# Attention values by split single-pass products on five of eight key tiles, and an unsplit key product

## The chip, the cores and the metric

The kernel runs on one core of one Trainium2 chip. Times are device microseconds (us) of one execution. The time before is 673.21 us, the median of 3 runs (672.68 to 674.67).

## The reference, cut to what matters

The computation is one gated cross-attention block and one feed-forward block. The change touches the attention alone:

```python
q_hk = (hidden_q @ Wq.T).reshape(b, s, H, K)              # hidden_q is the layer norm of x
q_big = jnp.einsum('bshk,hkq->bshq', q_hk, w_kc_q)
kv_rope = kv_c * cos[None] + _rotate_half(kv_c) * sin[None]
q_r = jnp.einsum('bshq,hqr->bhsr', q_big, W_qr)
k_r = jnp.einsum('bld,hdr->bhlr', kv_rope, W_kr)           # the key product
scores = jnp.einsum('bhsr,bhlr->bhsl', q_r, k_r)
attn = jax.nn.softmax(scores, axis=-1)
ctx_c = jnp.einsum('bhsl,bld->bhsd', attn, kv_rope)        # the value product
ctx_lat = jnp.einsum('bhsd,hkd->bshk', ctx_c, w_kc_kv)
out = ctx_lat.reshape(b, s, H * K) @ Wo.T
```

There are 2 batches of 512 queries and 1024 keys, 16 heads, a key and value width of 128. The feed-forward part that follows has quantized weights of 512 x 2048 and runs in FP8 and BF16.

## The kernel before

**Pairs, units, steps.** Heads are taken two at a time: eight pairs, p = 0 to 7. A pair has four units, w = 0 to 3: unit w serves batch w // 2 and one half of its queries. A unit has eight steps, c = 0 to 7. In step c TensorE multiplies key tile c (128 keys) of the softmax by the values (`pv_matmul`), and adds it into one PSUM bank, `ps_ctx` for even units and one bank of `ps_b` for odd ones. Between the steps lie the side tasks of `SIDE`: `m` and `a` make the next pair's query matrix, `q` its queries, `k` its keys (`k_hi`, `k_lo`), `b` the pair's output matrix, and `out` applies it. All orders are written out by hand, one queue for each engine. An engine works its queue strictly in order, and semaphores order the engines among themselves.

**One unit's softmax runs ahead.** For a unit two or three units ahead, PE makes the scores of query tiles t = 2, 3 in step 1 and of t = 0, 1 in step 5 (`score_matmuls`). For each tile VectorE (DVE) takes the maximum from PSUM (`max_tile`), ScalarE (ACT) the exponential into `E` (`exp_tile`), DVE the reciprocal of the row sum (`inv_tile`), GpSimd (POOL) scales the tile (`pool_scale`), and DVE turns its 32 x 32 blocks in place (`turn_blocks`). Scores for two more tiles can be written only when both exponentials of the last two are done. When a unit's four tiles are turned, SyncE (SP) issues 16 transfers that exchange partition groups from `E` to `G` (`exchange`). `G` then holds the turned softmax, the moving operand of `pv_matmul`. The buffers `E`, `G` and the result banks have two places, for even and odd units.

**Two ways to multiply float32.** PE multiplies plain float32 in one instruction of the program, which the trace shows as two records. The other way splits each operand x into a high part, x rounded to the one-pass format fp32r, and a low part x - high, and adds three one-pass products: high by high, high by low, low by high. ACT copies out the high part, and DVE (for PSUM) or POOL (for SBUF) subtracts for the low part. Scores, outputs, the keys (`k`) and in pairs 1 to 4 the queries (`q`) are split. The value product, `m`, `a` and `b` are plain.

**Names.** `ctx_high` and `ctx_low` split a unit's result. `side_high` and `side_low` split a side task's. `wk_high` and `wk_low` split the key weights and `kvT_hi`, `kvT_lo` are the split transposed values, used for the keys. In pairs 0 to 3 ACT also sums the absolute values of the feed-forward weights (`sum_half`, one half at steps 1 and 4). From unit 1 of pair 4 it takes two halves' tanh in step 0 (`tanh_half`), and DVE rounds them in steps 3 and 4 (`round_half`). I call pairs 0 to 3 the summing pairs and pairs 4 to 6 the rounding pairs. In pair 0 POOL makes the low parts of the layer-normed input (`xn_low`, four halves), for which PE waits before pair 1; in pairs 4 and 5 it joins them again (`join_xn`).

Of the kernel before, what the change touches and what calls it, by code (L numbers as in the profile page):

```python
# [99 lines left out]
WK_AT = (0, 1)  # L100
# [81 lines left out]
def build(nc, A):  # L182
    with ExitStack() as ctx:
# [947 lines left out]
        def _(sp):  # L1131
# [35 lines left out]
        def xn_low(pool, b):  # L1167

            pool.wait_ge(side_done, side_index(0, "first", ("q", b)) + 1)
            for i in (2 * b, 2 * b + 1):  # L1170
                hi, lo, full = xn_half(i)
                pool.wait_ge(xn_high, i + 1)
                nc.gpsimd.tensor_tensor(lo, full, hi.bitcast(F32), ALU.subtract).then_inc(xn_split, 1)

        def join_xn(pool, b):
# [2 lines left out]
            for h in range(2):
                hi, lo, _ = xn_half(2 * b + h)
                whole = xn_rows[:, b, h * DT // 2:(h + 1) * DT // 2, :].rearrange("p c s -> p (c s)")  # L1180
                nc.gpsimd.tensor_tensor(whole, hi.bitcast(F32), lo.bitcast(F32), ALU.add).then_inc(xn_joined, 1)

        def pool_pair(pool, p, last=False):
            for w in range(4):
                second, first = not (last and w >= 2), not (last and w >= 1)
                for at, t in enumerate((1, 2, 3, 0)):
                    if second if t else first:
                        pool_scale(pool, *unit_ahead(p, w, 2 if t else 3), t)
                    if at == 0:
                        if is0(p) and w in XN_LOW_SLOTS:  # L1190
                            xn_low(pool, XN_LOW_SLOTS.index(w))
                        for b in range(BATCH):
                            if isinstance(p, int) and (p, w) == XN_JOIN_SLOTS[b]:
                                join_xn(pool, b)
                    if last and (w, at) == (1, 2):
                        ln2_root(pool, 0)
                if last and w == 1:
                    atanh_end(pool)
# [8 lines left out]
        @block.gpsimd
        def _(pool):
# [788 lines left out]
```

## Time and profile before

| | before |
|---|---|
| median of the runs | 673.21 us |
| profiled execution | 677.15 us, span 675.4 us |
| mean granted TensorE clock | 0.995 |
| busy: PE, DVE, ACT, POOL | 653.5, 543.9, 356.8, 259.7 us |

Times below are counted in us from the start of the span. A matmul record overlaps the next one, so what a matmul costs is read from start to start. ACT's and DVE's records overlap the next by about 0.1 us as well. A pair starts with its first value tile, just ahead of task `m`: `m` of pairs 1 to 6 starts at 116.99, 182.95, 248.93, 316.5, 383.13 and 451.25. The feed-forward part begins about 561.

### The profile page before, as it was taken

The page shows a single profiled execution, that of the slowest core. Times are in us where ns is not written, and L with a number is a line of the kernel's source. Part 1 is how long each engine was busy: PE and PEld are TensorE (multiplying, and loading weights), DVE is VectorE, ACT ScalarE, POOL GpSimd, SP SyncE. Part 2 cuts the span into 40 slices and gives each one's busy share as a digit, 9 for nine tenths or more (in the row PEclk, how much of TensorE's full clock was granted, in tenths as well). Part 3 has the DMA queues.
Part 4 walks back from the last instruction along what each step waited for, and adds up shares of the span by engine and source line. Part 5 has one row for each costly group of instructions (what it writes and reads, how often), then busy time and mean ns, then how long its engine had stood idle before and what let it go on. Part 6 is the DMA issues. An engine that isn't in the chain of part 4 may idle for free.

```text
span 675.4 us, 9297 instructions
## 1 busy us (share of the span) xinstructions
PE 653.5 (97%) x2870; PEld 377.5 (56%) x2870; DVE 543.9 (81%) x882; ACT 356.8 (53%) x571; POOL 259.7 (38%) x232
## 2 busy tenths in 40 slices
PE   9798999999999999999999999999999898999997
PEld 8564555665665555565655555555555454445553
DVE  5787877788868885888698979997999886998873
ACT  3564664455445544554545454545454533498875
POOL 4822265133223222322235443332333352686651
PEclk9999999999999999999999999999999998999999
DMA  8108885788498849884988688869688763000001
GB/s 299 63 1 218 234 226 117 226 237 228 108 241 243 220 105 243 231 215 109 239 245 207 184 225 237 212 168 238 163 214 230 172 149 101 1 0 32 17 33 48
DMA packets 45206, 112.77 MB, mean 167 GB/s; under 512 B 11888, under 2 KB 15088, under 8 KB 45040
## 3 DMA queue, kind: packets, MB, share of 16 engines
q1 hardware_dynamic: 43712, 110.01, 61.5%
q10 hardware_dynamic: 1392, 2.29, 1.0%
q8 instruction: 19, 0.31, 0.2%
q14 instruction: 19, 0.16, 0.1%
q0 software_dynamic: 64, 0.00, 0.0%
HBM read 45.16 MB, written 2.10 MB: 70 GB/s over the span
## 4 chain that ended last, share of the span: by engine, by line
PE 48%; DVE 30%; ACT 7%; SPq 6%; POOL 3%; issue 3%; DMA 2%; PEld 1%; POOLq 0%; DVEq 0%; ACTq 0%; PEldq 0%
DVE E L1765 9%; PE ps_b L1392 9%; PE ps_s L1371 7%; DVE small L1755 7%; PE ps_ctx L1392 7%; ACT E L1580 6%; SPq L1096 5%; PE ps_s L586 5%; DVE wq L1781 2%; PE ps_b L1265 2%; POOL E L1160 2%; DVE x_sb L1745 2%; PE ps_b L1267 2%; PE ps_b L637 2%; PE ps_b L1266 2%
## 5 line engine op out<-in xcount | busy, mean ns | idle before, releaser
L1160 POOL TENSOR_SCALAR E<-E,small 128x1024 f32<-128x1024 f32 x128 | 151.1, 1190 | 346.7 <-DVE small L1760 346.6
L1580 ACT ACTIVATE E<-ps_s,small 128x1024 f32<-128x1024 f32 x128 | 142.3, 1113 | 209.0 <-DVE small L1755 177.5
L1765 DVE STREAM_TRANSPOSE E<-E 128x1024 f32<-128x1024 f32 x124 | 152.8, 1233 | 27.9 <-POOL E L1160 27.8
L1755 DVE TENSOR_REDUCE small<-ps_s 128x1 f32<-128x1024 f32 x128 | 149.1, 1203 | 4.5 <-PE ps_s L1371 4.4
L1392 PE MATMUL ps_ctx<-G,kv 128*128 128x512 f32 x256 | 123.2, 599 | 0.0
L1392 PE MATMUL ps_b<-G,kv 128*128 128x512 f32 x256 | 119.9, 598 | 2.1 <-DMA G<-E 2.1
L1392 PEld LDWEIGHTS ps_b<-G,kv 128*128 128x128 f32 x256 | 48.0, 190 | 51.8 <-issue 46.0
L1392 PEld LDWEIGHTS ps_ctx<-G,kv 128*128 128x128 f32 x256 | 46.4, 189 | 43.0 <-issue 40.3
L1265 PE MATMUL ps_b<-b_hi,ctx_hi 128*128 128x512 f32 x128 | 66.4, 519 | 0.6 <-DVE ctx_lo L1717 0.6
L1371 PE MATMUL ps_s<-k_hi,q_hi 64*128 64x512 f32 x256 | 57.3, 443 | 4.6 <-ACT E L1580 3.6
L586 PE MATMUL ps_s<-wq,q12T 128*128 128x512 fp8e4 x256 | 61.1, 385 | 0.1
L1371 PE MATMUL ps_s<-k_hi,q_lo 64*128 64x512 f32 x256 | 51.1, 393 | 0.0
L1371 PE MATMUL ps_s<-k_lo,q_hi 64*128 64x512 f32 x256 | 50.8, 392 | 0.0
L1267 PE MATMUL ps_b<-b_lo,ctx_hi 128*128 128x512 f32 x128 | 50.4, 393 | 0.0
L1266 PE MATMUL ps_b<-b_hi,ctx_lo 128*128 128x512 f32 x128 | 50.2, 392 | 0.0
L524 POOL TENSOR_TENSOR hg<-h_f,E 128x512 f32<-128x512 f32 x32 | 40.4, 1270 | 25.1 <-DVE h_f L932 25.1
L1745 DVE SCALAR_TENSOR_TENSOR x_sb<-ps_b,small,x_sb 128x512 f32<-128x512 f32 x62 | 44.6, 720 | 4.7 <-PE ps_b L1267 4.7
L1760 DVE RECIPROCAL small<-small 128x1 f32<-128x1 f32 x128 | 19.3, 156 | 31.0 <-ACT E L1580 24.7
L1371 PEld LDWEIGHTS ps_s<-k_hi,q_hi 64*128 64x128 f32 x256 | 24.1, 183 | 32.6 <-issue 19.1
L586 PEld LDWEIGHTS ps_s<-wq,q12T 128*128 128x128 bf16 x256 | 24.4, 99 | 28.3 <-issue 4.1
L1265 PEld LDWEIGHTS ps_b<-b_hi,ctx_hi 128*128 128x128 f32 x128 | 24.0, 188 | 23.1 <-issue 15.3
L1266 PEld LDWEIGHTS ps_b<-b_hi,ctx_lo 128*128 128x128 f32 x128 | 24.1, 189 | 10.5 <-issue 7.7
(199 smaller groups left out, 960.9 us busy)
## 6 DMA issues: line engine op xcount, KB each, us to landing
G<-E SPq DMA_DIRECT2D x496, 128.0 KB, 2.4
w_stage<-in_wffn SPq DMA_DIRECT2D x48, 512.0 KB, 4.4
wo_s<-in_woT SPq DMA_DIRECT2D x8, 512.0 KB, 5.3
wq_s<-in_wq SPq DMA_DIRECT2D x7, 512.0 KB, 6.3
wkcq_s<-in_wkcqT SPq DMA_DIRECT2D x7, 384.0 KB, 4.5
out<-x_sb SPq DMA_DIRECT2D x8, 256.0 KB, 2.0
x_sb<-in_x SPq DMA_DIRECT2D x3, 512.0 KB, 5.9
wqr_s<-in_wqr SPq DMA_DIRECT2D x7, 192.0 KB, 5.4
```

What stands on the lines that cost most here:

```text
L524: nc.gpsimd.tensor_tensor(hg[:, k, cols], h_f[:, k, cols], g3[:, cols], ALU.mult).then_inc(hg_done, 1)
L586: last = nc.tensor.matmul(ps_s4[:, 2 * i + c % 2, :], q12T[:, k, i, d, :], wq8[:, DT * i + d, cols], start=(d == 0), stop=(d == DT - 1))
L1160: nc.gpsimd.tensor_scalar(e, e, rowinv[:, k:k + 1], 1.0, ALU.mult, ALU.mult).then_inc(scaled, 1)
L1265: nc.tensor.matmul(into, ctx_hi[:, cols], b_hi[:, h, :], start=(h == 0), stop=False)
L1266: nc.tensor.matmul(into, ctx_lo[:, cols], b_hi[:, h, :], start=False, stop=False)
L1267: last = nc.tensor.matmul(into, ctx_hi[:, cols], b_lo[:, h, :], start=False, stop=(h == 1))
L1371: last = nc.tensor.matmul(ps_s[:, h, cols], q[head, b, rows], k[head, b, cols], start=(i == 0), stop=(i == 2))
L1392: last = nc.tensor.matmul(CTX_PS[w % 2].rearrange("p (t i q) -> p t i q", t=ST, i=4), kv[:, w // 2, c, :], turned, start=(c == 0), stop=(c ...
L1580: nc.scalar.activation(out, scores, ACT.Exp, bias=negmax[:, k:k + 1], accum_out=rowsum[:, k:k + 1]).then_inc(exp_done, 1)
L1745: last = nc.vector.scalar_tensor_tensor(x, bank_in, g_tanh[:, 0:1], x, ALU.mult, ALU.add)
L1755: nc.vector.tensor_reduce(negmax[:, k:k + 1], ps_s[:, t % 2, :], AX_X, ALU.max, negate=True).then_inc(max_done, 1)
L1765: nc.vector.transpose(e_tile(w % 2, t), e_tile(w % 2, t)).then_inc(blocks_turned, 1)
```

## The change

Five of the eight value tiles of a unit (`SPLIT = 5`, tiles 0 to 4) are multiplied as three one-pass products in pairs 0 to 6. The values' parts `kv_hi`, `kv_lo` are cut once by POOL in the prologue. The softmax's high part is copied by ACT (`split_high`) into one of three places of `g_hi`, and POOL (`split_low`) puts the low part into the memory of `G` itself. PE takes the tiles in the order of `STEP_TILE`, so that each unit opens with a plain tile. Pair 7 takes all tiles plain, for which POOL adds the values together again (`join_kv`). The key product becomes plain, so the split of `kvT` and of the key weights falls away (one `wk` copy on ACT and one subtraction on DVE in a pair, four subtractions on DVE in the prologue), and the next key weights are loaded later. `xn_low` and `join_xn` are taken one half at a time, at the end of a unit's POOL work.

```diff
+SPLIT = 5
+HIGH_PLACE = (0, 2, 1, 0, 1)
+STEP_TILE = (5, 0, 6, 1, 2, 3, 7, 4)
+HIGH_STEPS = (0, 0, 0, 2, 4)
-WK_AT = (0, 1)
-XN_AT = ((1, 1), (1, 4), (2, 1), (2, 4))
-XN_LOW_SLOTS = (2, 3)
+XN_AT = ((1, 1), (1, 5), (2, 1), (2, 5))
+XN_LOW_SLOTS = (1, 2, 3, 3)
-XN_JOIN_SLOTS = ((4, 2), (5, 0))
+XN_JOIN_SLOTS = ((4, 2), (4, 3), (5, 0), (5, 0))
...
+        def split_low(pool, p, w, i):
+            tile = g_tile(w % 2, i)
+            pool.wait_ge(split_hi, SPLIT * 4 * p + (SPLIT * w + i + 1))
+            pool.sem_inc(pool_passed, 1)
+            nc.gpsimd.tensor_tensor(g_tile(w % 2, i, G_lo), tile, high_part(i).bitcast(F32).rearrange("p (t i q) -> p t i q", t=ST, i=4),
+                                    ALU.subtract).then_inc(split_lo, 1)
...
+                u2, u3 = unit_ahead(p, w, 2), unit_ahead(p, w, 3)
+                if is0(p) and w == 0:
+                    split_low(pool, p, w, 0)
+                if second:
+                    pool_scale(pool, *u2, 1)
...
+                if not (last or is0(p) and w == 0):
+                    split_low(pool, p, w, 0)
+                if not last:
+                    split_low(pool, p, w, 1)
...
+                if not last:
+                    split_low(pool, p, w, 2)
+                if second:
+                    pool_scale(pool, *u2, 2)
+                    pool_scale(pool, *u2, 3)
...
+                    split_low(pool, p, w, 3)
...
+                    split_low(pool, p, w, 4)
+                for i in range(2 * BATCH):
+                    if is0(p) and w == XN_LOW_SLOTS[i]:
+                        xn_low(pool, i)
+                    if isinstance(p, int) and (p, w) == XN_JOIN_SLOTS[i]:
+                        join_xn(pool, i)
+                if isinstance(p, int) and (p, w) == (PAIRS - 2, 3):
+                    join_kv(pool, 0)
+                if first:
+                    pool_scale(pool, *u3, 0)
...
-                nc.tensor.matmul(into, wh, kvT_hi[:, b, cols], start=True, stop=False)
-                nc.tensor.matmul(into, wl, kvT_hi[:, b, cols], start=False, stop=False)
-                last = nc.tensor.matmul(into, wh, kvT_lo[:, b, cols], start=False, stop=True)
+                last = nc.tensor.matmul(into, wkr_s[:, :, :].rearrange("p a r -> p (a r)"), kvT[:, b, cols], start=True, stop=True)
...
+            if tile < SPLIT and not (isinstance(p, int) and p == PAIRS - 1):
+                high = high_part(tile).rearrange("p (t i q) -> p t i q", t=ST, i=4)
+                pe.wait_ge(split_lo, SPLIT * 4 * p + (SPLIT * w + tile + 1))
+                nc.tensor.matmul(into, kv_hi[:, b, tile, :], high, start=(c == 0), stop=False)
+                nc.tensor.matmul(into, kv_lo[:, b, tile, :], high, start=False, stop=False)
+                last = nc.tensor.matmul(into, kv_hi[:, b, tile, :], g_tile(w % 2, tile, G_lo), start=False, stop=(c == LT - 1))
+                if tile < SPLIT - 1:
+                    last.then_inc(split_done, 1)
+            else:
+                last = nc.tensor.matmul(into, kv[:, b, tile, :], turned, start=(c == 0), stop=(c == LT - 1))
...
+        def split_high(act, p, w, i):
+            used = 4 * (SPLIT - 1) * p + (SPLIT - 1) * w
+            if i == 0:
+                if is0(p) and w == 0:
+                    act.wait_ge(kv_cut, 6)
+                else:
+                    act.wait_ge(split_done, used)
+                act.wait_ge(exchanged[w % 2], 2 * EXCHANGE * p + EXCHANGE * (w // 2 + 1))
+            elif i == 2:
+                if not (is0(p) and w == 0):
+                    act.wait_ge(pv_done, 4 * p + w)
+            elif i == 3:
+                act.wait_ge(split_done, used + 1)
+            elif i == 4:
+                act.wait_ge(split_done, used + 3)
+            copy_act(high_part(i).rearrange("p (t i q) -> p t i q", t=ST, i=4), g_tile(w % 2, i)).then_inc(split_hi, 1)
...
+                    if c == 0 and variant != "last":
+                        split_high(act, p, w, 0)
                     if c == 0 and w:
                         ctx_high(act, p, w - 1)
...
-                    if (w, c) == WK_AT and variant != "last":
-                        wk_high(act, 16 * p + 32)
+                    for i in range(1, SPLIT):
+                        if c == HIGH_STEPS[i] and variant != "last":
+                            split_high(act, p, w, i)
```

ACT's queue around the start of unit 2 of pair 4, before. `ctx_hi` is the result of unit 1, the first `k_hi` the last key task of unit 1, `w_stage` the two tanh halves, the second `k_hi` the key task of step 0, `E` the four exponentials of the unit, and the last `ctx_hi` opens unit 3:

```order
L1536 ACTIVATE ctx_hi<-ps_b 128x512
L1536 ACTIVATE k_hi<-ps_b 128x512
L1604 ACTIVATE w_stage<-w_stage,small 128x1024 x2
L1536 ACTIVATE k_hi<-ps_b 128x512
L1580 ACTIVATE E,small<-ps_s,small 128x2x4x128 x4
L1536 ACTIVATE ctx_hi<-ps_ctx 128x512
```

The same place in the changed kernel:

```order
L1615 ACTIVATE g_hi<-G 128x512
L1615 ACTIVATE ctx_hi<-ps_b 128x512
L1615 ACTIVATE k_hi<-ps_b 128x512
L1615 ACTIVATE g_hi<-G 128x512 x2
L1698 ACTIVATE w_stage<-w_stage,small 128x1024 x2
L1615 ACTIVATE k_hi<-ps_b 128x512
L1674 ACTIVATE E,small<-ps_s,small 128x2x4x128
L1615 ACTIVATE g_hi<-G 128x512
L1674 ACTIVATE E,small<-ps_s,small 128x2x4x128
L1615 ACTIVATE g_hi<-G 128x512
L1674 ACTIVATE E,small<-ps_s,small 128x2x4x128 x2
```

Three copies now stand ahead of the tanh halves and so of the second `k_hi`, and one stands between the exponentials of query tiles 2 and 3.

POOL's queue from the middle of pair 0 to its end, before. `xnT` are the low parts of the input, `E` the scalings, and the branch opens the loop over pairs 1 to 3:

```order
L1160 TENSOR_SCALAR E<-E,small 128x4x256 x14
L1173 TENSOR_TENSOR xnT<-xn_rows,xnT 128x1024 x2
L1160 TENSOR_SCALAR E<-E,small 128x4x256 x4
L1173 TENSOR_TENSOR xnT<-xnT_full,xnT 128x1024 x2
L1160 TENSOR_SCALAR E<-E,small 128x4x256 x3
L1253 UNCONDITIONAL_BRANCH
```

In the changed kernel, units 2 (end) and 3 of pair 0:

```order
L1194 TENSOR_TENSOR xnT<-xn_rows,xnT 128x1024
L1182 TENSOR_SCALAR E<-E,small 128x4x256 x2
L1226 TENSOR_TENSOR G_lo<-G,g_hi 128x4x4x32 x3
L1182 TENSOR_SCALAR E<-E,small 128x4x256 x2
L1226 TENSOR_TENSOR G_lo<-G,g_hi 128x4x4x32 x2
L1194 TENSOR_TENSOR xnT<-xnT_full,xnT 128x1024 x2
L1182 TENSOR_SCALAR E<-E,small 128x4x256
L1324 UNCONDITIONAL_BRANCH
```

The last two low parts of the input, which stood ahead of three scalings of unit 3, now stand behind two of them and behind the unit's five value-tile subtractions.

## Rows read from the trace of the kernel before

**Rows 1.** Windows, pairs 2 and 5: busy PE, PEld, DVE, ACT, POOL; granted clock; DMA.

```profile
182.95:248.93 65.98, 65.98 (x279) 39.77 (x278) 52.51 (x73) 32.41 (x58) 17.84 (x17) 1.00 0.78 203
383.13:451.25 68.12, 67.96 (x269) 37.97 (x268) 58.91 (x81) 34.54 (x57) 25.81 (x19) 1.00 0.80 213
```

**Rows 2.** Chain that ended last, pair 2: start us, us, what.

```profile
226.38 1.59 PE ps_s L1371 x12
```

**Rows 3.** The same chain, pair 5, unit 2.

```profile
424.49 1.14 DVE small L1755
...
425.66 2.35 ACT E L1580 x4
...
428.03 0.06 DVE small L1760
```

**Rows 4.** Timeline of PE, pair 2: plain value tiles, then split query products.

```profile
229.40 2.73 PE L1392 MATMUL ps_ctx<-G,kv 128*128 128x512 f32 x6
...
231.97 1.02 PE L1392 MATMUL ps_b<-G,kv 128*128 128x512 f32 x2
...
233.06 0.40 PE L1345 MATMUL ps_b<-xnT,a_lo 128*128 128x512 f32 x1
...
235.34 0.39 PE L1346 MATMUL ps_b<-xnT,a_hi 128*128 128x512 f32 x1
```

**Rows 5.** Timeline of ACT, pair 5: copies.

```profile
401.65 0.60 ACT L1536 ACTIVATE ctx_hi<-ps_ctx 128x512 fp32r<-128x512 f32 x1
...
402.12 0.61 ACT L1536 ACTIVATE b_hi<-ps_b 128x512 fp32r<-128x512 f32 x1
...
422.59 0.58 ACT L1536 ACTIVATE k_hi<-ps_b 128x512 fp32r<-128x512 f32 x1
```

**Rows 6.** Timeline of DVE, pair 5.

```profile
387.89 0.42 DVE L1717 TENSOR_TENSOR wk_lo<-wkr_s,wk_hi 128x128 fp32r<-128x128 f32 x1
...
411.58 0.16 DVE L1760 RECIPROCAL small<-small 128x1 f32<-128x1 f32 x1
...
411.74 1.36 DVE L1781 TENSOR_SCALAR wq<-w_stage 128x1024 fp8e4<-128x1024 f32 x1
...
423.84 0.65 DVE L1717 TENSOR_TENSOR k_lo<-ps_b,k_hi 128x512 fp32r<-128x512 f32 x1
...
427.05 0.69 DVE L1781 TENSOR_SCALAR wq<-w_stage 128x1024 fp8e4<-128x1024 f32 x1
...
428.03 0.16 DVE L1760 RECIPROCAL small<-small 128x1 f32<-128x1 f32 x1 [0.28 <-ACT E L1580]
```

**Rows 7.** Timelines of ACT and PE, pair 2 (first row) and pair 3.

```profile
224.74 1.12 ACT L1580 ACTIVATE E<-ps_s,small 128x1024 f32<-128x1024 f32 x1
...
265.22 1.11 ACT L1580 ACTIVATE E<-ps_s,small 128x1024 f32<-128x1024 f32 x1 [7.47 <-DMA G<-E]
...
268.79 0.50 PE L1344 MATMUL ps_b<-xnT,a_hi 128*128 128x512 f32 x1 [1.10 <-DVE b_lo L1717]
...
292.38 1.12 ACT L1580 ACTIVATE E<-ps_s,small 128x1024 f32<-128x1024 f32 x1
...
293.65 0.50 PE L1371 MATMUL ps_s<-k_hi,q_hi 64*128 64x512 f32 x2
```

**Rows 8.** Groups of POOL and ACT by form: busy us, mean ns, idle before.

```profile
L524 POOL TENSOR_TENSOR hg<-h_f,E 128x512 f32<-128x512 f32 x32 | 40.4, 1270 | 25.1 <-DVE h_f L932 25.1
...
L1173 POOL TENSOR_TENSOR xnT<-xnT_full,xnT 128x1024 fp32r<-128x1024 f32 x2 | 4.7, 2375 | 1.6 <-PE ps_b L1341 1.6
...
L1536 ACT ACTIVATE xnT<-xn_rows 128x1024 fp32r<-128x1024 f32 x2 | 2.1, 1052 | 0.0
```

**Rows 9.** Timelines of PE and ACT in pair 0, and the chain at its end.

```profile
52.05 0.50 PE L1371 MATMUL ps_s<-k_hi,q_hi 64*128 64x512 f32 x2 [0.37 <-ACT E L1580]
...
107.79 1.11 ACT L1580 ACTIVATE E<-ps_s,small 128x1024 f32<-128x1024 f32 x1
...
116.13 0.86 PE ps_ctx L1392 x2
```

More of the change, by code:

```diff
@@ L1124, in sp_pair @@
                     load_wq(sp, p + 2)
-                    sp.wait_ge(wk_ready, p + 2)
+                if w == 2 and not (variant == "last" or isinstance(p, int) and p == 6):
+                    sp.wait_ge(side_done, side_index(p, variant, ("k", 1, 1)) + 1)
                     load_kr(sp, p + 2)
@@ L1165, in xn_half, with xn_low @@
             return tuple(x.rearrange("p c s -> p (c s)") for x in (XNT[b][:, 0, part, :], XNT[b][:, 1, part, :], XNT_FULL[b][:, part, :]))
[L1167 to L1175, printed above, removed]
-            pool.wait_ge(side_done, side_index(XN_JOIN_PAIR, "mid", ("q", b)) + 1)
[L1178 to L1181, printed above, removed]
+        def xn_low(pool, i):
+            pool.wait_ge(side_done, side_index(0, "first", ("q", i // 2)) + 1)
+            hi, lo, full = xn_half(i)
+            pool.wait_ge(xn_high, i + 1)
+            nc.gpsimd.tensor_tensor(lo, full, hi.bitcast(F32), ALU.subtract).then_inc(xn_split, 1)
@@ L1185, in pool_pair @@
                 second, first = not (last and w >= 2), not (last and w >= 1)
[L1186 to L1198, printed above, removed]
+                u2, u3 = unit_ahead(p, w, 2), unit_ahead(p, w, 3)
[3 more added lines that the diff above has]
+                    pool_scale(pool, *u2, 1)
+                if last and w == 0:
+                    join_kv(pool, 1)
+                if not (last or is0(p) and w == 0):
+                    split_low(pool, p, w, 0)
+                if not last:
+                    split_low(pool, p, w, 1)
+                if last and w >= 2:
+                    ln2_root(pool, w - 2)
+                if last and w == 3:
+                    rms_root(pool, 1)
+                if not last:
[3 more added lines that the diff above has]
+                    pool_scale(pool, *u2, 3)
                 if last and w == 2:
@@ L1248, in _ @@
                 pool_scale(pool, 0, 0, t)
-            for t in range(ST):
-                pool_scale(pool, 0, 1, t)
+            cut_kv(pool, 0)
+            pool_scale(pool, 0, 1, 0)
+            pool_scale(pool, 0, 1, 1)
+            cut_kv(pool, 1)
+            pool_scale(pool, 0, 1, 2)
+            pool_scale(pool, 0, 1, 3)
             pool_scale(pool, 0, 2, 0)
@@ L1315, in side_matmuls @@
                 _, b, j = task
-                pe.wait_ge(wk_ready, 1 if at is not None else p + 2)
+                pe.wait_ge(ld_kr, 16 if at is not None else 16 * p + 32)
                 if at is not None:
@@ L1821, in dve_pair @@
                         inv_tile(dve, *u3, 0)
-                    if (w, c) == WK_AT and variant != "last":
-                        wk_low(dve, p + 2)
                     if variant == "last":
```

87 lines of the change are left out of this document (50 added, 37 removed).

## The prediction

> **What bounds the kernel now.** I read the busy times of whole pairs first. PE is busy for 65.98 of 65.98 us in summing pair 2, and for 67.96 of 68.12 in rounding pair 5 [rows 1], at a granted clock of 1.00, the level of 2.4 GHz. That looks like one bound for the whole attention. Yet a busy share does not say who waits for whom, and DVE rises from 52.51 to 58.91 us between the two pairs.
>
> So I read the chain that ended last. In pair 2 it is PE work alone, one matmul group behind the other [rows 2]. In pair 5 hardly a matmul stands in it: maximum on DVE, exponentials on ACT, reciprocal on DVE, then rounding and turning on DVE [rows 3]. The reader should see that 0.28 us of DVE's waiting ahead of a reciprocal is for an exponential of ACT [rows 6], while PE, the busiest engine, sets nothing there. From about 329 to 547 us the chain keeps that shape. The kernel thus has two regimes: pairs 0 to 3 (to 316) by PE, pairs 4 to 7 by the softmax chain through DVE and ACT.
>
> Last I looked for how much room the softmax chain has in the PE regime. In pair 3 the exponentials of the step 6 scores wait 7.47 us for the exchange of unit 1, and behind them PE waits 1.10 us for `b_lo` at 268.79. In unit 2 the exponential that starts at 292.38 ends at 293.50, and the scores that need its bank start at 293.65. In pair 2 the same exponential ends at 225.86 and the scores start at 226.31. The room is 0.15 and 0.45 us [rows 2, 7].
>
> **PE's own account.** Six records of plain tiles, three products, take 231.97 - 229.40 = 2.57 us, 0.857 each. Ten steps of split products take 235.34 - 233.06 = 2.28, 0.228 each, so 0.684 for three [rows 4]. A split product saves 0.173 us. There are 5 x 28 = 140 of them, 24.2 us. The plain key product costs 0.173 more, 32 times: 5.5. PE's work falls by 18.7 us, 2.8 in a pair. The low part is read from `G` in pieces of 32 columns. Plain tiles are read in the same pieces, at 0.214 us for each 512-column quarter, so I charge nothing for it.
>
> The Trainium skill, page "Perfetto Trace Analysis", section "Identifying the Most-Contended Engine", says to find the bottleneck by occupancy and to optimize that engine first, with a warning that matmul busy share is a poor measure. By the plain rule the sum would be 673.2 - 18.7 = 654.5. The chain's row decides against it for pairs 4 to 6.
>
> **What is added elsewhere.** ACT gets 140 copies. A copy of 512 columns costs 0.47 from start to start [rows 5], and one of 1024 from SBUF 1.05 [rows 8]: I take 0.5. POOL gets 140 subtractions of 1.27 [rows 8]. Both engines have the time: 32 to 35 us and 18 to 26 us of 66 to 68 are busy [rows 1], and 10 and 25 come on top. What counts is where they stand.
>
> *Rounding pairs.* The copy of tile 3 stands between the exponentials of query tiles 2 and 3. In unit 2 DVE waits for the second one already, so all 0.5 goes into the chain. In unit 1 the reciprocal at 411.58 follows rounding at once [rows 6] and the exponential ends just then, so 0.5 there too, and by the same pattern in unit 3. In unit 0 it is 0.5 less the `wk_lo` that goes, a record of 0.42 [rows 6] that overlaps the next by the usual 0.1: 0.15 to 0.2. Three more copies stand ahead of the tanh halves, and ACT comes to `k_hi` or `q_hi` 1.5 us later. `k_hi` ends at 423.17 [rows 5] and `k_lo` takes it at 423.84 [rows 6], 0.67 of room: DVE stalls 0.8, and the maxima stand behind it. Unit 3 repeats this with `q_hi` and `q_lo`. In unit 1 the query product itself ends later than that, in unit 0 there is no such task. A pair: 0.15 + 0.5 + 1.3 + 1.3 = 3.25 us. Pair 4 has no tanh in unit 0, and its exchange covers that unit: 3.1. In unit 0 of pair 5 two joins of 2.4 each [rows 8] stand ahead of a scaling and nearly fit: 0.3. Together 3.1 + 3.55 + 3.25 = 9.9. What PE saves here only becomes waiting.
>
> *Summing pairs 1 to 3.* From the landing of unit 1's exchange (265.2) a DVE chain runs to the scores of unit 2 at 293.65, with 0.15 us of room at the end. PE gets ready earlier there, but can't start earlier. Behind that point lie two split tiles of unit 2 and five of unit 3 before the next pair: 7 x 0.173 = 1.2 saved. The copy in unit 2 costs 0.5 less the room of 0.15 to 0.45, and unit 3's room takes most of its own. Pair 3: 0.6 saved. Pairs 1 and 2 have more room: 1.1 each. Together 2.8.
>
> *Pair 0.* In unit 0 tile 0 comes ahead of the scores, which now start at 52.05 [rows 9]. It needs ACT's copy behind exponentials that end about 52.0, a subtraction and three products: 0.5 + 1.3 + 0.7 = 2.5 us later. Bounds are 0 and 2.5. The next exponentials of that unit wait for the exchange anyway, as in pair 3, so I take half, 1.3. At the end, PE may not enter pair 1 before the last `xn_low`. The last exponential of unit 3 ends at 108.9 [rows 9], now 1.3 + 0.5 + 0.5 later, 111.2. Reciprocal and scaling end at 112.5, two subtractions at 115.0, two `xn_low` of 2.4 at 119.8. PE enters at 116.13 now: 3.7 us lost in pair 0, the 1.3 included.
>
> *The rest.* In the prologue `cut_kv` is six POOL operations of 640 columns, by the rate of 1.27 for 512 at most 1.6 each, in two gaps of POOL ahead of scalings; the four `kvT_lo` go, and four plain key products come. I put zero, with 1 us either way. Pair 7 has no copies. `join_kv`, up to 1.6 us on POOL twice, lies ahead of scalings that wait for exponentials: zero.
>
> **Sum:** 3.7 - 2.8 + 9.9 = 10.8 us. The profiled execution took 677.15 (span 675.4), and would take 688. The median of the runs is 3.9 lower, and on it the forecast is 684.0. Since nearly all of it is latency, its own range is 678 to 690: less if half the copies on the chain are covered, more if pair 0's opening is not.
>
> **Rivals.**
> *PE stays the bound and gains (faster).* If the chain has more room than I read, so that the copies cost nothing, pairs 0 to 3 gain about 2.3 each, 9, and pairs 4 to 6 stay: 664. It decides where the room ahead of the scores in unit 2 exceeds 0.5 + 0.5 us, PE's saving and the copy; the 0.15 of rows 7 speaks against it, PE's full busy time for it. All of 18.7 gained would be 654.5. Chance 0.27, a third of it below 664.
> *The two sides cancel.* The entry of pair 1 is not delayed and the copies cost half: -2.8 + 5 is 675. Chance 0.08 within 0.3%.
> *The port.* Rounding takes 0.69 alone and 1.36 beside a POOL scaling [rows 6]. If POOL's subtractions meet the first rounding of each unit too, 11 roundings grow by 0.67, and some turn into POOL delays: 7 more, 691. Against it: the three subtractions ahead of the scaling should be over by then. The Trainium skill, page "SBUF — State Buffer", section "Who interferes with whom", has the pair of ports taken for a whole instruction, and two-input DVE operations from SBUF meet POOL's reads too; the rows agree as to rounding. Chance 0.10, together with a slower read of the low parts.
> *The forecast:* 0.55.
>
> **How the numbers follow.** What a measurement of this kernel can tell from no change is about 0.3%, 2 us. Slower: 0.55 + 0.10 = 0.65; same 0.08; faster 0.27. The range from 664 to 690 leaves out a tenth on each side.
>
> **What the profile would show.** Right: PE idle of several us in each of pairs 4 to 6, before scores, released by ACT's exponentials; these pairs 71 us long; `k_lo` waiting for `k_hi` in unit 2; PE idle about 3 us where pair 1 opens, waiting for POOL's `xnT`; key products of 0.857 and split ones of 0.23. Wrong: pairs 4 to 6 at 68 or shorter, or pairs 1 to 3 below 64. The forecast fails if ACT reaches the copies before the exponentials are ready, or if the queue has slack that the overlapping records hide.

## The result, and the profile after

| | before | after |
|---|---|---|
| median of the runs | 673.11 us (4 runs, 672.68 to 674.67) | 686.43 us (4 runs, 685.49 to 688.11) |
| ratio | | 1.0196, 95% interval 1.0168 to 1.0225 |
| profiled execution | 677.15 us, span 675.4 | 685.49 us, span 683.7 |
| mean granted clock of the executions, here and below | 0.994 to 1.00 | 0.982 to 0.99 |

The change costs 13.3 us. A second measurement of the changed kernel, below, gave 1.0184 (1.0154 to 1.0213).

The page of the changed kernel: busy times (share of the span, instructions), the engines' shares of the chain that ended last, and five of the costliest groups (busy us, mean ns, idle time ahead and its releaser).

```profile
PE 643.2 (94%) x2978; PEld 398.7 (58%) x2978; DVE 536.9 (79%) x870; ACT 425.3 (62%) x703; POOL 443.3 (65%) x380
...
DVE 37%; PE 21%; ACT 17%; issue 13%; POOL 7%; SPq 3%; DMA 1%; DVEq 0%; POOLq 0%; PEld 0%; ACTq 0%
...
L1226 POOL TENSOR_TENSOR G_lo<-G,g_hi 128x512 fp32r<-128x512 f32 x140 | 176.8, 1291 | 0.4 <-ACT g_hi L1615 0.4
...
L1615 ACT ACTIVATE g_hi<-G 128x512 fp32r<-128x512 f32 x140 | 84.6, 628 | 0.6
L1438 PE MATMUL ps_s<-k_hi,q_hi 64*128 64x512 f32 x256 | 57.9, 447 | 14.2 <-ACT E L1674 13.2
...
L1472 PE MATMUL ps_ctx<-G,kv 128*128 128x512 f32 x116 | 59.8, 609 | 3.5 <-POOL xnT L1194 3.2
...
L1466 PE MATMUL ps_ctx<-g_hi,kv_hi 128*128 128x512 f32 x70 | 42.4, 605 | 8.5 <-POOL G_lo L1226 8.2
```

From the page of the kernel before, the row of the scores:

```profile
L1371 PE MATMUL ps_s<-k_hi,q_hi 64*128 64x512 f32 x256 | 57.3, 443 | 4.6 <-ACT E L1580 3.6
```

PE's busy time fell by 10.3 us (653.5 before), and the span grew by 8.3. PE is still busy for 94% of it, but only 21% of the chain is PE's, where it was 48%. PE now idles 14.2 us ahead of scores instead of 4.6, nearly all of it for ACT's exponentials, and 8.5 ahead of split tiles for POOL's low parts.

The windows of pairs 0 to 2 and 5 (columns as in [rows 1]):

```profile
48.30:124.83 76.53, 67.63 (x277) 41.05 (x275) 54.60 (x73) 50.78 (x91) 54.22 (x43) 0.94 0.68 176
124.83:190.47 65.64, 64.55 (x294) 43.08 (x293) 51.09 (x70) 39.74 (x72) 40.86 (x35) 0.99 0.78 205
190.47:255.83 65.36, 63.87 (x293) 42.58 (x292) 52.02 (x71) 41.88 (x78) 42.86 (x37) 1.00 0.80 205
390.01:459.71 69.70, 65.92 (x285) 40.99 (x284) 57.28 (x79) 43.76 (x74) 50.56 (x39) 1.00 0.79 208
```

Pair 2 took 65.98 us with PE always busy [rows 1]; now it takes 65.36 with 1.5 idle. Pair 5 took 68.12, now 69.70 with 3.8 idle. Pair 0 is the bad one: 76.53, with 8.9 idle and a granted clock of 0.94.

From the start of each pair's first `m` record to the next one's (the last column to the first record of the feed-forward part's matmuls), in us, one profiled execution each. The kernels from the third row on are those of the experiments:

| kernel | pair 0 | 1 | 2 | 3 | 4 | 5 | 6 and 7 |
|---|---|---|---|---|---|---|---|
| before | 68.4 | 66.0 | 66.0 | 67.6 | 66.8 | 68.1 | 110.7 |
| after | 76.5 | 65.6 | 65.4 | 66.3 | 67.9 | 69.7 | 112.2 |
| changed_again | 76.1 | 66.4 | 65.3 | 66.2 | 67.9 | 69.7 | 112.6 |
| copy_behind | 74.7 | 65.6 | 64.6 | 65.7 | 67.6 | 69.0 | 111.5 |
| copies_after_k | 74.9 | 65.2 | 65.3 | 66.1 | 66.6 | 68.1 | 111.0 |
| late_xn_wait | 71.4 | 67.6 | 65.3 | 66.2 | 67.9 | 69.7 | 113.2 |
| open_tile6 | 70.5 | 66.2 | 65.5 | 66.4 | 67.9 | 70.3 | 113.1 |
| open_filled | 75.0 | 67.5 | 65.3 | 66.2 | 67.9 | 70.2 | 112.8 |
| rounding_plain | 75.0 | 66.4 | 65.3 | 66.2 | 66.6 | 68.0 | 110.8 |
| key_alone | 68.8 | 66.6 | 66.6 | 66.8 | 67.4 | 68.3 | 111.5 |
| all_four | 67.4 | 67.6 | 66.0 | 65.8 | 66.5 | 67.5 | 110.0 |
| combo_round_plain | 67.4 | 67.7 | 64.8 | 65.7 | 66.6 | 68.0 | 111.3 |
| five | 67.8 | 65.3 | 64.7 | 65.8 | 66.4 | 67.6 | 109.9 |
| copy_between | 68.6 | 66.2 | 65.4 | 66.1 | 66.7 | 68.1 | 110.4 |

Rows that leave a pair alone differ there by up to 2 us in pairs 0 and 1 and by some tenths elsewhere; that is how finely the table can be read.

**Pair 0's opening.** Timeline of PE in the changed kernel: the plain tile 5, tile 0, then the scores (start us, us, ..., idle before and releaser).

```profile
49.64 1.02 PE L1472 MATMUL ps_ctx<-G,kv 128*128 128x512 f32 x2
53.90 0.55 PE L1466 MATMUL ps_ctx<-g_hi,kv_hi 128*128 128x512 f32 x1 [3.24 <-POOL G_lo L1226]
...
55.24 0.80 PE L1438 MATMUL ps_s<-k_hi,q_hi 64*128 64x512 f32 x2
55.83 0.63 PE L1438 MATMUL ps_s<-k_lo,q_hi 64*128 64x512 f32 x2
```

The scores start 3.19 us later than the 52.05 of [rows 9], and behind the gap every score step takes 0.43 us from start to start instead of 0.23: the granted clock is at its 1.2 GHz level there.

The next exponentials on ACT, before and in the changed kernel, and a second wait of PE in the same unit, for the low part of tile 3:

```profile
64.55 1.11 ACT L1580 ACTIVATE E<-ps_s,small 128x1024 f32<-128x1024 f32 x1 [5.81 <-DMA G<-E]
```

```profile
67.77 1.11 ACT L1674 ACTIVATE E<-ps_s,small 128x1024 f32<-128x1024 f32 x1 [4.03 <-DVE small L1847]
```

```profile
66.60 0.50 PE L1466 MATMUL ps_ctx<-g_hi,kv_hi 128*128 128x512 f32 x1 [1.95 <-POOL G_lo L1226]
```

**Pair 0's end.** The same timeline, and POOL's row for the last low parts of the input.

```profile
119.41 0.40 PE L1468 MATMUL ps_b<-G_lo,kv_hi 128*128 128x512 f32 x1
122.97 2.07 PE L1472 MATMUL ps_ctx<-G,kv 128*128 128x512 f32 x2 [3.16 <-POOL xnT L1194]
124.83 2.01 PE L1372 MATMUL ps_b<-wqr_s,wkcq_s 128*128 128x128 f32 x12
```

```profile
117.95 4.68 POOL L1194 TENSOR_TENSOR xnT<-xnT_full,xnT 128x1024 fp32r<-128x1024 f32 x2
```

Again PE is slow behind the gap: a plain tile takes 1.86 us to the next start instead of 0.857.

**Rounding pairs.** Timeline of DVE, unit 2 of pair 5, the place of [rows 3, 6].

```profile
432.00 0.69 DVE L1813 TENSOR_TENSOR k_lo<-ps_b,k_hi 128x512 fp32r<-128x512 f32 x1 [0.71 <-ACT k_hi L1615]
432.61 2.35 DVE L1847 TENSOR_REDUCE small<-ps_s 128x1 f32<-128x1024 f32 x2
435.10 0.16 DVE L1852 RECIPROCAL small<-small 128x1 f32<-128x1 f32 x1
435.25 0.69 DVE L1873 TENSOR_SCALAR wq<-w_stage 128x1024 fp8e4<-128x1024 f32 x1
436.71 0.16 DVE L1852 RECIPROCAL small<-small 128x1 f32<-128x1 f32 x1 [0.77 <-ACT E L1674]
436.87 0.70 DVE L1873 TENSOR_SCALAR wq<-w_stage 128x1024 fp8e4<-128x1024 f32 x1
```

`k_lo` waits 0.71 for `k_hi`, and the second reciprocal 0.77 where it waited 0.28 [rows 6]. But the rounding behind it takes 0.70. Before, it took 1.11:

```profile
428.18 1.11 DVE L1781 TENSOR_SCALAR wq<-w_stage 128x1024 fp8e4<-128x1024 f32 x1
```

### The profile page after: what moved, and what is told of

Same layout as the page of the kernel before. It is cut to its first block, busy times and chain, and to the rows that moved or that the text cites. A ratio compares the mean times of both kernels' runs of the same rounds, so it can differ in the third digit from the quotient of the medians.

```text
span 683.7 us, 10097 instructions
## 1 busy us (share of the span) xinstructions
PE 643.2 (94%) x2978; PEld 398.7 (58%) x2978; DVE 536.9 (79%) x870; ACT 425.3 (62%) x703; POOL 443.3 (65%) x380
## 4 chain that ended last, share of the span: by engine, by line
DVE 37%; PE 21%; ACT 17%; issue 13%; POOL 7%; SPq 3%; DMA 1%; DVEq 0%; POOLq 0%; PEld 0%; ACTq 0%
DVE small L1847 12%; DVE E L1857 10%; ACT E L1674 9%; PE ps_s L607 5%; POOL E L1182 4%; DVE x_sb L1841 3%; SPq L1117 3%; ACT g_hi L1615 3%; PE ps_s L1438 2%; PE ps_b L1408 2%; PE ps_b L658 2%; ACT w_stage L1698 2%; DVE wq L1873 2%; DVE ctx_lo L1813 1%; DVE k_lo L1813 1%
## 5 line engine op out<-in xcount | busy, mean ns | idle before, releaser
L1226 POOL TENSOR_TENSOR G_lo<-G,g_hi 128x512 fp32r<-128x512 f32 x140 | 176.8, 1291 | 0.4 <-ACT g_hi L1615 0.4
L1615 ACT ACTIVATE g_hi<-G 128x512 fp32r<-128x512 f32 x140 | 84.6, 628 | 0.6
L1438 PE MATMUL ps_s<-k_hi,q_hi 64*128 64x512 f32 x256 | 57.9, 447 | 14.2 <-ACT E L1674 13.2
L1472 PE MATMUL ps_ctx<-G,kv 128*128 128x512 f32 x116 | 59.8, 609 | 3.5 <-POOL xnT L1194 3.2
L1472 PE MATMUL ps_b<-G,kv 128*128 128x512 f32 x116 | 58.7, 594 | 2.1 <-DMA G<-E 2.1
L1336 PE MATMUL ps_b<-b_hi,ctx_hi 128*128 128x512 f32 x128 | 56.7, 443 | 1.0 <-DVE ctx_lo L1813 0.5
L545 POOL TENSOR_TENSOR hg<-h_f,E 128x512 f32<-128x512 f32 x32 | 40.5, 1274 | 23.3 <-DVE h_f L953 23.3
L1438 PEld LDWEIGHTS ps_s<-k_hi,q_hi 64*128 64x128 f32 x256 | 24.5, 185 | 44.9 <-issue 22.1
L1466 PE MATMUL ps_ctx<-g_hi,kv_hi 128*128 128x512 f32 x70 | 42.4, 605 | 8.5 <-POOL G_lo L1226 8.2
L1466 PE MATMUL ps_b<-g_hi,kv_hi 128*128 128x512 f32 x70 | 42.5, 607 | 0.0
L607 PEld LDWEIGHTS ps_s<-wq,q12T 128*128 128x128 bf16 x256 | 24.1, 98 | 27.7 <-issue 3.2
```

Of the source, the lines that this page charges most:

```text
L607: last = nc.tensor.matmul(ps_s4[:, 2 * i + c % 2, :], q12T[:, k, i, d, :], wq8[:, DT * i + d, cols], start=(d == 0), stop=(d == DT - 1))
L1226: nc.gpsimd.tensor_tensor(g_tile(w % 2, i, G_lo), tile, high_part(i).bitcast(F32).rearrange("p (t i q) -> p t i q", t=ST, i=4), ALU.subtra ...
L1336: nc.tensor.matmul(into, ctx_hi[:, cols], b_hi[:, h, :], start=(h == 0), stop=False)
L1438: last = nc.tensor.matmul(ps_s[:, h, cols], q[head, b, rows], k[head, b, cols], start=(i == 0), stop=(i == 2))
L1466: nc.tensor.matmul(into, kv_hi[:, b, tile, :], high, start=(c == 0), stop=False)
L1472: last = nc.tensor.matmul(into, kv[:, b, tile, :], turned, start=(c == 0), stop=(c == LT - 1))
```

## The experiments

Where no other kernel is named, the edit is made to the changed kernel. Ratios are to the kernel before in the same session, and differences in us are differences of ratios by 673 us; each ratio is known to about 0.003, 2 us.

### The changed kernel again

No edit.

> The changed kernel itself, once more, so that the variants have it on the same chip and in the same hour: ratio 1.0196 as measured before, within its interval of 1.017 to 1.0225, pair 0 between 75 and 76.5 us long (three variants that leave it alone took 74.7 to 75.0).

Measured: 687.10 us, ratio 1.0184 (1.0154 to 1.0213). The differences below are taken from this ratio.

### The copy of tile 3 behind the exponentials

```diff
-HIGH_STEPS = (0, 0, 0, 2, 4)
+HIGH_STEPS = (0, 0, 0, 3, 4)
```

> Only the place of one copy changes: ACT takes the high part of value tile 3 behind the exponentials of query tiles 2 and 3 instead of between them (28 units). My prediction's account (copy on the chain): 0.5 us of the chain comes back in units 1 to 3 of pairs 4 to 6 and 0.15 in their units 0, 5 us, and in summing pairs 1 to 3 the wait of 0.96 us ahead of unit 2's scores shrinks by 0.5, 1.5 more: about 680, 6.5 below the 686.4 of the changed kernel. Rival (the copy was paid back): in the changed kernel's trace the second rounding of a unit takes 0.89 and 0.70 us where it took 1.36 and 1.11 before, since it no longer runs beside the scaling of tile 2. With the copy gone from its place rounding meets scaling again and grows by 0.4: only 0.1 per unit comes back, 1 us, and with the 1.5 of the summing pairs the time is about 684. The durations of the second rounding tell the two apart: 0.7 to 0.9 by the first, 1.1 to 1.36 by the rival.

Measured: 680.59 us, 1.0092 (1.0066 to 1.0118), 6.2 us less than the changed kernel. The size is that of the first theory, but the place is not. DVE in unit 2 of pair 5:

```profile
430.92 0.69 DVE L1873 TENSOR_SCALAR wq<-w_stage 128x1024 fp8e4<-128x1024 f32 x1
431.90 0.17 DVE L1852 RECIPROCAL small<-small 128x1 f32<-128x1 f32 x1 [0.28 <-ACT E L1674]
432.05 1.10 DVE L1873 TENSOR_SCALAR wq<-w_stage 128x1024 fp8e4<-128x1024 f32 x1
```

The reciprocal's wait is 0.28 again, and the second rounding 1.10 again, as the rival had it. From the first reciprocal to the end of the second rounding's issue (the next row's start, 433.07 here and 437.48 there) it takes 2.30 us, against 2.38 in the changed kernel. Against the changed kernel's second profile, pairs 4 to 7 got 2.0 us shorter, pairs 2 and 3 0.8 and 0.5. That is 3.3. Pairs 0 and 1 give 2.2 more in this execution, of which some is scatter of the clock (see the last section). So by the pairs the copy's place is worth more than the rival's 2.5 and less than the first theory's 6.5, and its 2.0 in pairs 4 to 7 are nearer to the rival's 1 than to the first theory's 5.

### The copies of tiles 1 and 2 behind k_hi and q_hi

```diff
-HIGH_STEPS = (0, 0, 0, 2, 4)
+HIGH_STEPS = (0, 1, 1, 2, 4)
```

> The copies of value tiles 1 and 2 move from step 0 to step 1 on ACT, behind the two tanh halves and behind k_hi or q_hi of step 0. My prediction's account: k_lo and q_lo wait 0.71 and 0.82 us for them in units 2 and 3 of pairs 4 to 6, and the maxima stand behind; the waits go, 2 x 0.75 x 3 = 4.5 us: about 682. Rival: the maxima would have waited anyway, for the scores or for the exchange, and the time stays at 686.4 within 1 us. A third way: low parts 1 and 2 come so late on POOL that the scaling of tile 2 is delayed, and the time rises by 1 to 3 us.

Measured: 681.41 us, 1.0112 (1.0083 to 1.0142), 4.8 us less. Pairs 4, 5 and 6 with 7 take 1.2, 1.6 and 1.6 us less, 4.4 together: the first theory's 4.5. `k_lo` no longer waits, in unit 2 of pair 5 (DVE):

```profile
426.67 0.65 DVE L1813 TENSOR_TENSOR k_lo<-ps_b,k_hi 128x512 fp32r<-128x512 f32 x1
427.24 2.34 DVE L1847 TENSOR_REDUCE small<-ps_s 128x1 f32<-128x1024 f32 x2
```

With this edit alone pairs 4 and 5 are as long as before the change (66.6 and 68.1).

### Pairs 4 to 6 with whole tiles

`split_high` and `split_low` are left out in pairs 4 to 6, and PE takes the plain product there (`splits` holds for pairs 0 to 3). The product reads the rounded high parts of the values; their low parts are left out.

```diff
-            if tile < SPLIT and not (isinstance(p, int) and p == PAIRS - 1):
+            if tile < SPLIT and splits(p):
```

> Pairs 4 to 6 take all value tiles whole again, without copies and subtractions; the low parts of the values of tiles 0 to 4 are left out there (the plain products read the rounded high parts). Pairs 0 to 3 as in the changed kernel. My prediction's account: the split costs 9.9 us in these pairs, of which the key product's saving and wk_low are a small part, so about 10 us come back: 676.5. Rival, from the two traces: pairs 4 and 5 grew only by 1.1 and 1.6 us and pairs 6 and 7 together by 1.5, so about 4 come back: 682.5.

Measured: 680.99 us, 1.0101 (1.0082 to 1.0121), 5.6 us less. The pairs themselves give 1.2, 1.7 and 1.8, 4.7 us. That is the rival's size, half of the 9.9 that I had forecast. The windows of pairs 4 and 5 (columns as in [rows 1]):

```profile
320.66:387.30 66.64, 66.64 (x274) 39.02 (x272) 57.54 (x80) 31.18 (x50) 23.89 (x19) 1.00 0.82 217
387.30:455.28 67.98, 67.98 (x266) 37.52 (x264) 58.51 (x79) 34.23 (x56) 25.87 (x19) 1.00 0.80 213
```

They are no shorter than with the copies of tiles 1 and 2 moved. But this doesn't show that these two copies are all that splitting cost the chain: with whole tiles and the plain key product PE is busy for the whole of both pairs, so here PE may be what holds them.

### Plain tile 6 ahead of tile 0 in the first unit

```diff
-            b, tile = w // 2, STEP_TILE[c]
+            b, tile = w // 2, ((5, 6, 0, 1, 2, 3, 7, 4) if is0(p) and w == 0 else STEP_TILE)[c]
```

> Only in unit 0 of pair 0 the value tiles are taken in the order 5, 6, 0 instead of 5, 0, 6, so that two plain tiles stand ahead of the scores and the scores need not wait for the low part of tile 0. Theory: the idle 3.24 us from 50.5 shrinks to at most 1, the scores start at about 52.1 instead of 55.24, and the granted clock does not fall; the unit loses 5 us against before, 3.2 by the idle time and 2 by the clock, and nearly all comes back: 682. Rival: what comes back is lost at the end of pair 0, where PE waits for the last low part of the input, whose start POOL reaches by its own chain; then the wait of 3.16 us there grows and the time falls by less than 2.

Measured: 681.51 us, 1.0100 (1.0073 to 1.0126), 5.6 us less. Timeline of PE at the opening:

```profile
51.79 0.51 PE L1438 MATMUL ps_s<-k_hi,q_hi 64*128 64x512 f32 x2 [0.32 <-ACT E L1674]
...
53.87 0.50 PE L1466 MATMUL ps_ctx<-g_hi,kv_hi 128*128 128x512 f32 x1 [0.42 <-POOL G_lo L1226]
```

Two gaps of 0.3 and 0.4 us stand in place of one of 3.24, and the score steps take 0.23. The query product of unit 1 starts 19.60 us after `m` (19.66 before, 24.89 after). A wait of 1.75 us for the low part of tile 3 stays, at 62.20, without moving the query product. The wait at the end of pair 0 stays as long as it was, 3.19 us, so the rival's return of the loss didn't come. Pair 0 is still 2.1 us longer than before the change.

### The gap at the opening filled with products

```diff
                         task_first = False
+                        wait_bank(pe, p, variant, ("a",))
+                        for _ in range(4):
+                            nc.tensor.matmul(ps_b[:, side_bank(variant, ("a",)), :]..., kv[:, 0, 5, :], g_tile(0, 5), start=True, stop=True)
                         pv_matmul(pe, p, w, c)
```

> The changed kernel with four plain products of tile 5 written to a free bank ahead of tile 0 in the first unit, so that TensorE works through its 3.24 us of waiting there (4 x 0.857 = 3.4 us); nothing else changes and their result is not used. If the loss behind the gap is the clock's: the granted clock stays at the 2.4 GHz level (1.00 in the window 48 to 60 instead of 0.72 to 0.85), the scores start at 55.3 as before but take 1.5 us instead of 2.6, the products behind them run at full speed, and pair 0 gets 2 us shorter: 684.5. If the clock has no part and only the wait counts, the time stays at 686.4.

Measured: 685.09 us, 1.0150 (1.0119 to 1.0180). That is 2.3 us under the changed kernel, with intervals that overlap. Windows of the changed kernel (second measurement), of this kernel, and of the kernel with the copies of tiles 1 and 2 moved, whose opening has a gap of 3.2 us that is not filled (length, busy PE, PEld, DVE, ACT, POOL, granted clock, DMA share, GB/s):

```profile
54.00:58.00 4.00, 4.00 (x16) 2.33 (x15) 0.20 (x1) 0.00 (x0) 2.76 (x3) 0.50 0.91 206
```

```profile
54.00:58.00 4.00, 4.00 (x27) 2.84 (x27) 2.17 (x2) 0.91 (x1) 2.78 (x3) 1.00 0.90 206
```

```profile
54.00:58.00 4.00, 4.00 (x27) 2.75 (x26) 2.07 (x2) 0.81 (x1) 2.88 (x3) 1.00 0.93 209
```

With the gap filled the clock behind it is 1.00, but in the third kernel it is 1.00 as well, with the gap. So this run doesn't show what lowers the clock. What the clock is worth can be read from the start of unit 1's query product after `m`: 24.9, 24.5, 24.3 and 24.1 us in the four executions whose clock fell right behind the gap (the changed kernel's two, copy_behind, late_xn_wait; in the first of them it fell behind the next gap as well), 23.3 and 23.4 in the two where it fell only behind the next gap (copies_after_k, rounding_plain), 23.4 here, where it fell there too. A fall at once costs 0.7 to 1.5 us more, and filling the gap brings nothing against those two. Of the 5.2 us lost in this unit, 3.6 or more are not the first fall's. The 2.3 us between the medians are within what the intervals leave open.

### The wait for the input's low parts moved to its user

```diff
-            pe.wait_ge(xn_split, 2 * BATCH)
             with pe.Fori(1, 4) as p:
...
                     else:
+                        pe.wait_ge(xn_split, 2 * BATCH)
                         for c in range(DT):
```

> PE's wait for the last low parts of the input moves from ahead of pair 1 to the query products of pairs 1 to 4, its first user, in unit 1. Theory: the idle 3.16 us ahead of pair 1 goes, and with it what the slow clock behind it cost (the first value tile 1.86 us instead of 0.86, m 1.94 instead of 1.4, some more until 128): about 5 us, 681.5. Rival: the softmax chain of pair 1 (exponentials, then the exchange) is what is late, PE only waits elsewhere, and at most 1 us comes back: 685.5 to 686.5.

Measured: 685.07 us, 1.0155 (1.0125 to 1.0184), 2.0 us less. Neither theory: pair 0 is 4.7 us shorter and pair 1 is 1.3 longer. PE's timeline in pair 1:

```profile
124.66 0.50 PE L1467 MATMUL ps_ctx<-g_hi,kv_hi 128*128 128x512 f32 x1 [2.54 <-POOL G_lo L1226]
```

PE enters pair 1 at once, and then stands for tile 0, whose low part is behind the same `xn_low` in POOL's queue. The wait moved 4 us on and shrank by 0.6.

### The plain key product alone

The kernel before, with the key product of the change and without the split of the key weights and of the transposed values. The value tiles stay plain.

> The kernel before with only the plain key product (no split of the transposed values and of the key weights, the later load of them), and no split value tiles. Account by PE work: 0.173 x 4 a pair, 0.7 us in each of the PE-bound pairs 0 to 3 and nothing in pairs 4 to 6 but the saving of wk_low (0.15 a pair): 2.8 - 0.5 = 2.3 slower, 675.5. Rival: the wk copy on ACT and subtraction on DVE were on the chain, and in the prologue four subtractions on DVE; then it is even or faster, 671 to 673.

Measured: 677.91 us, 1.0038 (1.0018 to 1.0058), 2.6 us slower, against the account's 2.3. The sum fits, but by the pairs it is not made up as the account has it. Pairs 0, 1 and 2 grow by 0.5, 0.6 and 0.6 us, near the 0.7 expected. Pair 3 gets 0.7 shorter, and pairs 4 to 7, which were to gain 0.5, grow by 1.6. In pair 5 PE is busy for 68.22 of 68.30 us.

### The four edits together

`HIGH_STEPS = (0, 1, 1, 3, 4)`, tile 6 ahead of tile 0, and the late wait for the low parts.

> The four edits together: copies of tiles 1 and 2 in step 1, the copy of tile 3 behind both exponentials, the wait for the low parts of the input at the query products, and plain tile 6 ahead of tile 0 in the first unit. If the four are independent and each returns what the account gives it (6.5, 4.5, 5, 4.5), 666; if the copies were paid back by shorter roundings and only pair 0's two waits and the summing pairs return, 686.4 - 5 - 4 - 1.5 = 676. Below 673 it beats the kernel before.

Measured: 671.36 us, 0.9958 (0.9945 to 0.9972). It is faster than the kernel before. The four edits alone sum to 18.6 us (6.2 + 4.8 + 5.6 + 2.0), together they bring 15.2.

### The four edits, and pairs 4 to 6 whole

The low parts of the values are left out in pairs 4 to 6, as above.

> The four edits together, and pairs 4 to 6 with whole value tiles (the low parts of the values of tiles 0 to 4 left out there). If the summing pairs keep PE's saving once the waits are gone, pairs 1 to 3 take 63.2 to 63.9 us instead of 66 and pair 0 about 67: 673 - 8 - 1 = 664. Rival: the summing pairs are held by the softmax chain through unit 2 and stay at 65 or more: 669 to 671.

Measured: 672.97 us, 0.9967 (0.9952 to 0.9981), not to be told from the four edits alone. Pair 2 took 64.8 and pair 1 67.7: the first theory's 63.2 to 63.9 came nowhere. In pairs 4 and 5 the four edits alone leave PE busy for 64.4 of 66.5 and 65.7 of 67.5 us, here for all of 66.6 and 68.0. So PE's saving in pairs 4 to 6 is worth 0.1 to 1.3 us in each column of the table, and nothing that the runs can tell.

### A fifth edit, and the copy put back between

```diff
                     split_low(pool, p, w, 2)
+                if is0(p) and w == 3:
+                    xn_low(pool, 2)
                 if second:
...
-                    if is0(p) and w == XN_LOW_SLOTS[i]:
+                    if is0(p) and w == XN_LOW_SLOTS[i] and i != 2:
```

> The four edits, and the third low part of the input taken in POOL's gap of 2 us ahead of the scaling of tile 2 in unit 3 of pair 0, instead of at the end of that unit. With the four edits PE still waits 1.91 us for the low part of tile 0 at 120.4 and runs at a lower granted clock behind it (0.86 in the window 120 to 132). Theory: POOL reaches that subtraction 2.4 us earlier, the wait goes, pair 1 takes 65.5 instead of 67.6 us, and the time is 669.3 (ratio 0.993). Rival: the scaling of tile 2 gets later by 0.4, the exchange of that unit with it, and nothing is gained: 671.4.

> As the kernel with five edits, but with the copy of tile 3 between the two exponentials again, as in the changed kernel. Alone, moving it behind them brought 1.7 us in pairs 4 to 7 (the second rounding went back from 0.70 and 0.89 to 1.10 and 1.38 us) and 0.6 to 0.8 in each of pairs 2 and 3. If these add to the other edits, this kernel is 2.5 to 3.5 us slower than the one with five edits; if the copy is now covered, the two are alike.

Measured: 671.49 us, 0.9952 (0.9934 to 0.9970) with the fifth edit. Pair 1 takes 65.3 us as expected, pair 0 0.4 more, and the profiled span is 669.2 against 672.2 of the four edits. The ratios are alike, though, so the fifth edit is not shown to bring anything. It is the fastest version by the ratio, 0.5% under the kernel before and 2.3% under the changed one. With the copy between the exponentials: 673.54 us, 0.9989 (0.9969 to 1.0008), 2.5 us slower, at the low end of what was expected of adding up.

## Why the prediction was right, and where it was not

The forecast of 684.0 is 2.4 us under the result, and the sign came from the named place: copies of ACT in a chain that PE's saving can't shorten. But the terms of the sum were off in opposite directions.

- **Two regimes, PE's saving turning into waiting.** Right in that PE's saving was of no use in pairs 4 to 6: with whole tiles there instead of split ones, the four edits lost nothing that the runs can tell. But the two limits lie close together, which the prediction didn't say. The softmax chain lets pairs 4 and 5 take 66.5 and 67.5 us with split tiles, and PE alone fills 66.6 and 68.0 with whole ones.
- **PE's saving, 18.7 us.** Mis-sized. Busy time fell by 2.1 us in pair 2 (65.98 to 63.87) and by 2.0 in pair 5 (67.96 to 65.92), where the account has 2.8 a pair. In all it fell by 10.3, as more of the work ran at the lower clock than before.
- **Key product.** Alone it costs 2.6 us against the 2.3 of the account. That is the right size, but 1.6 of it fell into pairs 4 to 7, where the account had a gain.
- **`k_lo` and `q_lo`, 0.8 us each.** The trace shows 0.71 and 0.82, and moving the copies brought 4.4 us in the pairs. Right.
- **The copy of tile 3, 0.5 a unit on the chain.** Failed as a term. The step was "in unit 2 DVE waits for the second one already, so all 0.5 goes into the chain". The wait did grow by 0.49 us, and the rounding behind it shrank from 1.11 to 0.70. Before, it started at 428.18, in the midst of POOL's scaling of tile 2 (427.26 to 428.74). Later by 0.5, it starts at 436.87, as that scaling ends (436.93). The Trainium skill, page "SBUF — State Buffer", section "Who interferes with whom", says of DVE's modes that use the port pair shared with GpSimd: whoever issues first holds the pair for its whole instruction. The rows fit that. In the prediction I had used this row only as a danger, and didn't ask what a delay of DVE does to the overlap. So the rounding pairs cost 4.2 to 4.7 us, not 9.9.
- **Summing pairs, 2.8 saved.** They saved 2.2 and, in the second measurement, 1.6. Right in kind, but not pair by pair: pairs 1 and 2 saved 0.3 and 0.6 where I had 1.1 each, and pair 3 saved 1.3 where I had 0.6. In pair 3 the kernel before waits 1.10 us for `b_lo` [rows 7], a wait that the changed kernel doesn't have, nor the one with the key product alone; whether it recurs in the kernel before, one profile can't say. In pair 2 PE's share is lost to new waits of 0.29 us for `G_lo` and 0.24 for `a_lo` in unit 0, and 0.96 for the exponential in unit 2, at the point that the room of [rows 7] had named.
- **Pair 0, 3.7 lost.** Mis-sized: it lost 8.2 us (76.53 - 68.37), 7.8 in the second measurement. The failed step is "the next exponentials of that unit wait for the exchange anyway, as in pair 3, so I take half". The opening cost 5.2 us by the start of the query product of unit 1 (24.89 - 19.66), above my bound of 2.5. The exchange covered nothing: the exponentials that waited for it at 64.55 start at 67.77, and now wait for DVE's maxima of the late scores. Before these scores PE waits 3.24 us, where I had 2.5 at most. The second wait of 1.95 us and the slow steps come on top, and the 2.23 us that PE had waited for `b_lo` ahead of the query product take some of it up. At the end PE waits until 122.97; I had 119.8. The opening's 3.9 us beyond my 1.3 account for that; POOL's order is as the prediction told it. With the opening mended (tile 6 ahead of tile 0) pair 0 loses 2.1 us, near the 2.4 that I had for its end.
- **The granted clock.** Missing from the sum. It falls in the units where PE has new gaps, and where it falls at once at the opening that costs 0.7 to 1.5 us more.

The sum of the corrections: pair 0 is 4.1 to 4.5 more, the rounding pairs 5.2 to 5.7 less, the summing pairs 0.6 to 1.2 more. They nearly cancel, and by the pairs the change costs 10.1 and 10.7 us in its two profiles, where I had 10.8. So the closeness of 684.0 is in large part luck. The profile of before was slow at the start of the feed-forward part (clock 0.80 and 0.77 in the windows from 560 to 568), which is part of its 4 us over its median; the changed kernel's lies 0.9 under its own. Hence 13.3 us between medians, and 8.3 between the profiled executions. What the medians have beyond the pairs' 10.1 to 10.7 is not shown.

Of the signs that I had set, the waits ahead of scores, ahead of `k_lo` and where pair 1 opens came. The pairs of 71 us did not: pair 4 took 67.9, which I had put down as a sign of being wrong, and pair 5 69.7.

The rival that PE gains (0.27) is refuted in its condition: room in unit 2 was under the copy's 0.5, and the scores waited 0.96 us. It was close to right about something else, though: a version with the same split and other places for the copies is faster than the kernel before. The port rival was backwards in sign: the 24 roundings together took 17.9 us where they had taken 22.1.

## What to carry to other kernels

Work moved off the busiest engine lands in the queues of others, and its price there is set by what stands behind each instruction: two copies of 0.5 us in front of `k_hi` and `q_hi` cost 4.4 us, twice what splitting saved in pairs 1 to 3. Before adding a delay on a shared resource, ask also which overlap it ends. When a chain holds a stage, ask how far below it the busiest engine's own limit lies: here it was a few tenths of a microsecond, so lowering only one of them could shorten the stage by no more than that. And look at the first unit of a pipeline on its own: there nothing runs ahead that covers a longer start, and behind a gap TensorE may run at the lower clock as well.

## What the runs showed of the hardware

**Idle gaps and the granted clock.** In the changed kernel's second measurement PE idles 1.78 us ahead of the scores in unit 2 of pair 4, and runs on at the 1.2 GHz level:

```profile
366.64 0.59 PE L1438 MATMUL ps_s<-k_hi,q_hi 64*128 64x512 f32 x2 [1.78 <-ACT E L1674]
367.01 0.64 PE L1438 MATMUL ps_s<-k_lo,q_hi 64*128 64x512 f32 x2
```

The same gap at 505.75 (1.78 us) was followed by slow steps in this execution, and in the first profiled one, at 506.20 (1.79 us), by none: the clock was 1.00 in all windows from 500 to 512. In pair 5 neither execution slowed behind its gap of 1.79 us (436.29 and 436.73). The opening's gap of 3.2 us was followed by a fall at once in four of the six profiled executions that have it, and in the other two the first fall came some 11 us later, behind the next gap, ahead of tile 3. With gaps of 0.3 and 0.4 us at the opening (open_tile6) there was none before 118. So what a gap costs differs from one execution to the next. In 4 us windows the changed kernel's clock was below 1.00 in four stretches up to its feed-forward part in both profiled executions, and in the kernel with five edits in none between 48 and 552 us; the timed executions agree, 0.982 to 0.99 against 0.997 to 1.00. How much of the 13.3 us is the clock's is not settled: no run held a gap and its clock apart, and part of the slow work lies where PE has room.

**A low part costs as much as it looks.** POOL's subtraction takes 1291 ns with its output in pieces of 32 columns, 1270 in whole rows [rows 8], and the reading of these pieces by PE shows little extra: three products take 0.70 us, against the 0.684 of [rows 4].
